# x by tokens and the output through 32x32 squares on VectorE instead of transposes on TensorE, in an attention and FFN kernel on one core

## The reference

```python
h = group_norm(x, 8 groups) * norm_w + norm_b
q, k, v = split(qkv_w @ h + qkv_b)
x = x + proj_w @ (softmax(q^T k / 16) v) + proj_b     # by tokens from here: t = x^T
n = layer_norm(t); u = n / |n|
t = t + softmax((u u^T)^2) @ n
y = layer_norm(t) @ (W - stop(W) + sign(W - mean W)) * mean|W| + bias
out = t + round(clip(y, -1, 1) * 7) / 7                # stored by channels again
```

## Time and profile before

| | |
|---|---|
| median of 3 runs | 1854.93 us (1854.73 to 1854.97) |
| profiled execution: its time, its span | 1856.45 us, 1854.7 us |
| granted TensorE clock | 0.998 of full speed |
| busy share PE, DVE, ACT, POOL | 99%, 68%, 49%, 52% |
| DMA | 35.42 MB, 16415 packets, mean 19 GB/s |

### The profile page before, as it was taken

How to read it: one execution, slowest core, us unless ns; L and a number is a source line. 1 busy time by engine, 2 the same in 40 slices (tenths; PEclk the granted TensorE clock), 3 DMA queues, 4 the chain that set the end, 5 groups by cost and what they waited for, 6 DMA issues and landing times.

```text
span 1854.7 us, 36871 instructions
## 1 busy us (share of the span) xinstructions
PE 1835.7 (99%) x12834; PEld 1699.1 (92%) x12834; DVE 1268.1 (68%) x2516; ACT 906.7 (49%) x1444; POOL 959.6 (52%) x2262
## 2 busy tenths in 40 slices
PE   7999999999999999999999999999999999999997
PEld 6999999989899998999989999999998999989997
DVE  6676766767666676666767667676676766767566
ACT  3545546445463544635446354454544536355452
POOL 0654727457274472734737356372654727447272
PEclk9999999999999999999999999999999999999999
DMA  2000010000100001000010100001000010000000
GB/s 77 1 24 24 1 45 0 23 23 0 45 0 23 23 0 45 0 34 11 0 45 0 45 0 10 35 0 45 0 23 23 0 45 0 23 23 0 24 1 23
DMA packets 16415, 35.42 MB, mean 19 GB/s; under 512 B 2688, under 2 KB 4096, under 8 KB 16384
## 3 DMA queue, kind: packets, MB, share of 16 engines
q1 hardware_dynamic: 16384, 35.01, 5.2%
HBM read 18.23 MB, written 16.78 MB: 19 GB/s over the span
## 4 chain that ended last, share of the span: by engine, by line
PE 98%; DVE 0%; DMA 0%; ACT 0%; SPq 0%; issue 0%; POOL 0%; ACTq 0%; POOLq 0%; DVEq 0%
PE wide L322 35%; PE narrow L424 8%; PE narrow L426 8%; PE narrow L425 8%; PE turn L434 6%; PE wide L424 5%; PE wide L426 5%; PE wide L425 5%; PE narrow L322 5%; PE wide L520 3%; PE turn L481 3%; PE turn L377 2%; PE narrow L452 2%; PE turn L511 1%; PE turn L528 1%; DMA qkv_b_c<-in_L_conv_qkv_b 0%
## 5 line engine op out<-in xcount | busy, mean ns | idle before, releaser
L322 PE MATMUL wide<-xn_hi,prob 128*128 128x512 f32 x1024 | 310.1, 404 | 0.0
L676 ACT ACTIVATE prob<-turn 128x1024 fp32r<-128x1024 f32 x128 | 131.3, 1026 | 322.0 <-PE turn L434 322.0
L1109 POOL TENSOR_TENSOR ln_v<-ln_mv,ln_eps 128x1 f32<-128x1 f32 x256 | 49.3, 193 | 428.8 <-DVE ln_mv L909 251.7
L891 DVE TENSOR_REDUCE neg_max<-wide 128x1 f32<-128x1024 f32 x128 | 156.4, 1222 | 123.0 <-PE wide L322 123.0
L690 ACT ACTIVATE ln<-tok,ln_shift,ln_r 128x256 f32<-128x256 f32 x128 | 77.2, 603 | 319.7 <-POOL ln_shift L1114 319.7
L424 PE MATMUL narrow<-prob 128*128 128x256 f32 x768 | 225.0, 293 | 0.0
L426 PE MATMUL narrow<-prob 128*128 128x256 f32 x768 | 217.0, 283 | 0.0
L425 PE MATMUL narrow<-prob 128*128 128x256 f32 x768 | 216.9, 282 | 0.0
L322 PEld LDWEIGHTS wide<-xn_hi,prob 128*128 128x128 f32 x1024 | 182.8, 188 | 35.4
L896 DVE TENSOR_TENSOR prob<-turn,prob 128x1024 fp32r<-128x1024 f32 x128 | 156.7, 1224 | 61.8 <-ACT prob L676 61.8
L669 ACT ACTIVATE expo<-wide,neg_max 128x1024 f32<-128x1024 f32 x128 | 142.5, 1113 | 58.2 <-DVE neg_max L891 58.1
(11 more groups left out here) (171 smaller groups left out, 5479.1 us busy)
## 6 DMA issues: line engine op xcount, KB each, us to landing
x_raw<-in_x SPq DMA_DIRECT2D x32, 512.0 KB, 3.9
out<-y_sb SPq DMA_DIRECT2D x32, 512.0 KB, 2.8
tok<-in_L_conv_qkv_w SPq DMA_DIRECT2D x1, 768.0 KB, 6.8
ln<-in_L_conv_proj_w SPq DMA_DIRECT2D x1, 256.0 KB, 6.8
ln<-in_L_ffn_weight SPq DMA_DIRECT2D x1, 256.0 KB, 3.0
out_bias<-in_L_conv_proj_b SPq DMA_DIRECT2D x1, 128.0 KB, 3.8
qkv_b_c<-in_L_conv_qkv_b SPq DMA_DIRECT2D x1, 3.0 KB, 7.4
norm_w_c<-in_L_conv_norm_w SPq DMA_DIRECT2D x1, 1.0 KB, 6.1
```

Source lines behind the costliest of these rows:

```text
L322: mm = pe.matmul(o, lhsT, r, start=first and i == 0, stop=last and i == len(parts) - 1)
L676: act.activation(eT_hi[:, n % 2], turn[:, :], ACT.Copy).then_inc(eT_hi_made, 1)
L891: dve.tensor_reduce(neg_max[:, n:n + 1], wide[n % 2][:, :], AX.X, ALU.max, negate=True).then_inc(max_made, 1)
```

## The change

x is no longer turned on TensorE. A second load brings it from DRAM already cut into squares of 32 channels by 32 tokens: partition 32 tq + cc of `x_quad` holds, for channel 32 cb + cc, the tokens 128 n + 32 tq to + 31 of each n. That takes 8 transfers (one for each cb) of 128 KB in rows of 128 bytes. ScalarE adds the bias of the channel (`bias_quad`, 8 instructions a batch, woven into `back`), and VectorE turns all 32x32 squares of half a batch with one transpose (`x_tokens`). The output goes the same way back: the FFN now gives tokens on partitions (its matmuls have the tokens' tile as the stationary side and 256 columns instead of 512), `ffn_out` moves to VectorE, `output` adds `tok` in SBUF and then turns squares into `out_quad`, which lies in the memory of `ln2`; 8 stores of 128 KB in rows of 128 bytes follow. The last batch's output is turned on TensorE (`turn_last`) and stored as before.

The diff, cut to what is spoken of below (`PLACES`, `LAST`: PSUM tiles of the loop and of the last batch):

```diff
+    xq_d = x.rearrange("b (cb cc) (n tq) w -> b tq cc cb n w", cc=Q, tq=P // Q)
+    outq_d = out.rearrange("b (cb cc) (n tq) w -> b tq cc cb n w", cc=Q, tq=P // Q)
...
+        out_quad = ln2[:, :, :].rearrange("p t c -> p (t c)").rearrange("p (cb n tt) -> p cb n tt", cb=C // Q, n=NT)
...
-            def store(f, hf):
-                sp.wait_ge(out_made, 2 * f + hf + 1)
-                sp.dma_start(out_d[f, :, :, hf * HALF:(hf + 1) * HALF], y_sb[:, hf]).then_inc(stored[hf], 16)
+            def load_quads(b):
+                for cb in range(C // Q):
+                    sp.dma_start(x_quad[:, cb], xq_d[b, :, :, cb]).then_inc(quad_loaded, 16)
+
+            def store(f):
+                sp.wait_ge(out_made, 2 * f + 2)
+                for cb in range(C // Q):
+                    sp.dma_start(outq_d[f, :, :, cb], out_quad[:, cb]).then_inc(stored, 16)
+
+            def store_last(hf):
+                sp.wait_ge(last_made[hf], 2)
+                sp.dma_start(out_d[B - 1, :, :, hf * HALF:(hf + 1) * HALF], out_last[:, hf]).then_inc(last_stored, 16)
...
+            load_quads(0)
             def reload(b):
-                sp.wait_ge(xT_up, 2 * b)
                 sp.wait_ge(xn_made, 2 * b)
                 load_x(b)
+            def reload_quads(b):
+                sp.wait_ge(xT_made, 2 * b)
+                load_quads(b)
+
             reload(1)
+            reload_quads(1)
             with sp.Fori(1, B - 1) as b:
                 reload(b + 1)
-                store(b - 1, 0)
-                store(b - 1, 1)
-            for f in (B - 2, B - 1):
-                store(f, 0)
-                store(f, 1)
-            sp.wait_ge(stored[0], 16 * B)
-            sp.wait_ge(stored[1], 16 * B)
+                reload_quads(b + 1)
+                store(b - 1)
+            store(B - 2)
...
-            def x_by_tokens(b, g):
-                if g:
-                    pe.wait_ge(xT_made, 2 * b + 1)
-                for t in range(HT):
-                    for k in range(KC):
-                        mm = pe.transpose(turn[:, t * C + k * P:t * C + (k + 1) * P],
-                                          x_raw[:, k, tile(HT * g + t)], ident[:, :])
-                mm.then_inc(xT_up, 1)
...
             def ffn(f, hf, places=PLACES):
                 pe.wait_ge(ln2T_made, 2 * f + hf + 1)
-                for m in range(KC):
+                for t in range(HT):
+                    o = places["y"][hf][t // 2][:, t % 2 * C:(t % 2 + 1) * C]
                     for k in range(KC):
                         for part in (tokT_lo, tokT_hi):
-                            mm = pe.matmul(places["y"][hf][m], sign_w[:, k, tile(m)],
-                                           part[:, k, hf * HALF:(hf + 1) * HALF],
+                            mm = pe.matmul(o, part[:, k, tile(HT * hf + t)], sign_w[:, k, :],
                                            start=k == 0 and part is tokT_lo, stop=k == KC - 1 and part is tokT_hi)
                 mm.then_inc(y_up, 1)
...
-            def turn_t(f, hf, places=PLACES):
+            def turn_last(hf):
+                pe.wait_ge(sum_made, 2 * (B - 1) + hf + 1)
                 for k in range(KC):
                     for t in range(HT):
-                        mm = pe.transpose(places["tT"][hf][:, k * HALF + t * P:k * HALF + (t + 1) * P],
-                                          tok[:, HT * hf + t, tile(k)], ident[:, :])
-                mm.then_inc(tT_up, 1)
+                        mm = pe.transpose(LAST["sum"][hf][:, k * HALF + t * P:k * HALF + (t + 1) * P],
+                                          y_sb[:, hf, t, tile(k)], ident[:, :])
+                mm.then_inc(last_up, 1)
...
-                    pe.wait_ge(pT_made, (NT - 1) * f + NT - 1)
-                x_by_tokens(b, 0)
-                if f is not None:
                     pe.wait_ge(t2_made, NT * f + NT - 1)
                 queries(b, 0)
-                x_by_tokens(b, 1)
                 if f is not None:
                     pe.wait_ge(t2_made, NT * f + NT)
                 else:
                     pe.wait_ge(prep_dve, 8)
                 queries(b, 1)
                 if f is not None:
-                    pe.wait_ge(xT_made, 2 * b + 2)
+                    pe.wait_ge(pT_made, (NT - 1) * f + NT - 1)
                     turn_ln2(f, 0)
...
-                    turn_t(f, 0)
-                    pe.wait_ge(y_made, 4 * f + 2)
+                    pe.wait_ge(y_made, 2 * f + 1)
                 scores1(b, 0)
                 if f is not None:
-                    pe.wait_ge(out_made, 2 * f + 1)
-                    turn_t(f, 1)
-                    pe.wait_ge(y_made, 4 * f + 4)
+                    pe.wait_ge(y_made, 2 * f + 2)
                 scores1(b, 1)
-                if f is not None:
-                    pe.wait_ge(out_made, 2 * f + 2)
-                else:
-                    pe.wait_ge(xT_made, 2 * b + 2)
                 turn_e1(b, 0)
...
+            def bias_quad(b, cb):
+                if cb == 0:
+                    act.wait_ge(quad_loaded, 16 * QUADS * (b + 1))
+                mm = act.activation(x_quad[:, cb], x_quad[:, cb], ACT.Identity, bias=quad_bias[:, cb, 0:1])
+                if cb == C // Q - 1:
+                    mm.then_inc(quad_biased, 1)
+
+            def layer_norm2(b, n, again=True):
                 act.wait_ge(ln2_scale, NT * b + n + 1)
+                if again and n == 0:
+                    act.wait_ge(stored, 16 * QUADS * b)
...
+                if f is None:
+                    act.wait_ge(quad_bias_made, 1)
+                    for cb in range(C // Q):
+                        bias_quad(0, cb)
...
+                    if more:
+                        bias_quad(b + 1, n)
...
             def x_tokens(b, g):
-                dve.wait_ge(xT_up, 2 * b + g + 1)
-                dve.tensor_tensor(x_tok[:, HT * g:HT * (g + 1), :],
-                                  turn[:, :].rearrange("p (t c) -> p t c", t=HT),
-                                  out_bias[:, :].unsqueeze(1).broadcast_to([P, HT, C]), ALU.add).then_inc(xT_made, 1)
+                dve.wait_ge(quad_biased, b + 1)
+                dve.transpose(x_tok[:, HT * g:HT * (g + 1), :].rearrange("p n (cb cc) -> p n cb cc", cc=Q),
+                              x_quad[:, :, HT * g:HT * (g + 1), :].rearrange("p cb n tt -> p n cb tt")
+                              ).then_inc(xT_made, 1)
...
+            def ffn_out(f, hf, places=PLACES):
+                dve.wait_ge(y_up, 2 * f + hf + 1)
+                wholes = [wide[hf][:, :]] if places is PLACES else places["y"][hf]
+                step = HT // len(wholes)
+                for i, whole in enumerate(wholes):
+                    last = dve.scalar_tensor_tensor(
+                        y_sb[:, hf, i * step:(i + 1) * step], whole.rearrange("p (t c) -> p t c", t=step),
+                        w_mean[:, 1:2], ffn_bias[:, :].unsqueeze(1).broadcast_to([P, step, C]), ALU.mult, ALU.add)
+                last.then_inc(y_made, 1)
...
+            def add_tokens(f, hf):
                 dve.wait_ge(q_made, 2 * f + hf + 1)
-                dve.tensor_tensor(y_sb[:, hf], places["tT"][hf][:, :].rearrange("p (k t) -> p k t", k=KC), y_sb[:, hf],
-                                  ALU.add).then_inc(out_made, 1)
+                dve.tensor_tensor(y_sb[:, hf], tok[:, HT * hf:HT * (hf + 1)], y_sb[:, hf], ALU.add).then_inc(sum_made, 1)
+
+            def output(f, hf):
+
+                add_tokens(f, hf)
+                dve.wait_ge(ln2T_up, 2 * f + 2)
+                dve.wait_ge(sum_made, 2 * f + hf + 1)
+                dve.transpose(out_quad[:, :, HT * hf:HT * (hf + 1)].rearrange("p cb n tt -> p n cb tt"),
+                              y_sb[:, hf].rearrange("p n (cb cc) -> p n cb cc", cc=Q)).then_inc(out_made, 1)
...
-                    output(f, 0)
                 row_max(b, 0)
-                if f is not None:
-                    output(f, 1)
                 row_max(b, 1)
                 e1T_lo(b, 0)
+                x_tokens(b, 0)
                 if more:
                     gn_sums(b + 1, 0)
                 for s in range(1, NT + 1):
@@ -1012,6 +1041,10 @@
                         e1T_lo(b, s)
                     if more and s == 1:
                         gn_sums(b + 1, 1)
+                    if s == 2:
+                        x_tokens(b, 1)
+                    if f is not None and s in (1, 4):
+                        output(f, s // 4)
...
+            ffn_out(f, 0, LAST)
             clip(f, 0)
             ln2T_lo(f, 1, LAST)
             quantise(f, 0)
-            output(f, 0, LAST)
+            ffn_out(f, 1, LAST)
             clip(f, 1)
+            add_tokens(f, 0)
             quantise(f, 1)
-            output(f, 1, LAST)
+            add_tokens(f, 1)
+            for hf in range(2):
+                dve.wait_ge(last_up, hf + 1)
+                dve.tensor_copy(out_last[:, hf, 1], LAST["sum"][hf][:, HALF:N]).then_inc(last_made[hf], 1)
```

(60 more changed lines are left out.)

20 lines of the change are left out of this document (11 added, 9 removed).

## The result

The changed kernel takes **1920.55 us** (1917.36 to 1923.79, 4 runs) against 1854.92: ratio 1.0354, 95% interval 1.0336 to 1.0372, 65.6 us slower, where 15 us faster was forecast. Its profiled execution took 1920.67 us for a span of 1919.0.

What follows compares the result with a forecast made beforehand. TensorE, busy 99% of the span, was taken as the bound; -54.6 (blocks) + 26 (VectorE's wait) + 10 (first batch) + 3.5 (tail) = -15 us gave 1840 us. Own range 1829 to 1850, with other cases 1824 to 2060.

Steps and rivals of the forecast that it cites:

- the sum: Whole kernel: -54.6 + 26 + 10 + 3.5 = -15 us, assuming blocks off TensorE shorten it unless another engine becomes late.
- Blocks, -54.6: TensorE: 62 blocks of 8 transposes leave, 0.88 us each, -54.6 us.
- VectorE's wait, +26: product1(b, 1) waits for residual1(b, 0) behind three new VectorE instructions, 1.75 us in each of 15 fronts, +26 us.
- First batch, +10: Prologue: squares land and ScalarE starts 8 biases at 39.5 us, first exponential at 44.5, +10 us.
- the prediction's own sign of being wrong: First batch: the prediction is wrong if the first exponential starts much before 44 us.
- Tail, +3.5: From the last FFN matmul's end to the last sum's end: 8.5 us instead of 5.0, +3.5 us.
- Transfers hidden: Rows of 128 bytes in the loop: 13 ns each on 4 engines, 53 us a batch, hidden with 18 us of room, 0.
- the prediction's count: Latest landing of a batch's stores before TensorE wants ln2: 926.8 us in the prediction, 1026.7 on e6's clock.
- slow rows: Rival: squares' rows slower than 17.5 ns, so the stores hold up ScalarE's back; decides from 17.8 ns; chance 0.35.
- dear transposes: Rival: a VectorE transpose takes 2.3 us, +35 and up to 10 more in step 4, 1875 to 1885 us; chance 0.10.
- The forecast of 1840: Whole kernel: 1854.9 - 15 = 1840 us, transfers hidden and VectorE's one wait; 1829 to 1850, chance 0.40.

Runs made afterwards that it cites:

- e6: Changed kernel with 28 more idle wait instructions on TensorE ahead of its first matmul: 1832.98 us.
- e9: e6 with the output's transposes moved to steps 3 and 5 (sums stay) and x_tokens(b, 0) put between row_max(b, 0) and row_max(b, 1): 1809.19 us.
- e8: e6 with output(f, 0) and output(f, 1) in steps 3 and 5 instead of 1 and 4: 1808.69 us.
- e11: e6 with 12 more loads of squares between a batch's eight loads and eight stores: 2029.6 us.
- e2: Changed kernel with 16 more idle wait instructions on TensorE ahead of its first matmul: 1925.33 us.
- e5: Changed kernel with 20 more idle wait instructions on TensorE ahead of its first matmul: 1924.49 us (2 runs).
- e10: e6 with 6 more loads of squares between a batch's eight loads and eight stores: 1833.47 us.
- e1: Changed kernel with 96 more idle wait instructions on TensorE ahead of its first matmul: 1837.38 us.
- e4: Changed kernel with each batch's eight loads and eight stores cut into rows of 1 KB, values in the wrong order: 1919.54 us.
- e3: Kernel before the change with 144 more idle wait instructions on TensorE ahead of its first matmul: 1905.38 us.
- e7: Changed kernel with 174 more idle wait instructions on TensorE ahead of its first matmul: 1864.5 us (1844.95 to 1870.99).

## Why the prediction was wrong, step by step

Starts of `product2` in the traces give a ledger (us; the end is that of the span):

| | first `product2` | period in the loop | last period | last `product2` to the end |
|---|---|---|---|---|
| before | 101.63 | 114.01 | 113.62 | 43.2 |
| after | 101.06 | 119.0 | 110.28 | 47.6 |
| e6 | 102.72 | 112.33 | 110.28 | 46.7 |
| e9 | 99.71 | 110.69 | 110.29 | 47.6 |

- **The step that failed** is the sum, by the sentence it starts from: "a block taken off TensorE shortens the kernel by its own length, as long as nobody else becomes late". Somebody did who is on no list of engines: TensorE's own instruction stream. Two blocks are 32 instructions out of the prologue (33 with a wait that went too), and the body's start moved from some 9 behind a block's border to 24 ahead of it. The sum has no term for that. From the first to the last `product2` the kernel after takes 1770.3 us and e6 1682.8: the missing term is **+87.4 us**, 6.7 a jump (the medians of the runs differ by 87.6). 51.1 of it are the waits. The other 36.3 go with the clock: it was at half in the loop for 12 stretches of 6.8 us and one of 3.4, 85 in all, of which some 19 are the second waits; half of the remaining 66 is 33, by my estimate.
- e6 starts 1.7 us later than the kernel after (102.72 against 101.06). Its 28 instructions are not the cause: e8, e9 and e11 have them too, and start at 99.7 to 100.1.
- The views that I read could have shown the risk only in part: the kernel before has 19 fetches on its page and none in its loop, which says that the body stays in place, but not by how little. The count of instructions would have said that some half of a block was left; where the borders lie took e2, e5 and e6 to find.
- *The instructions that stay.* In e6 no packet of `q8` comes between 206.1 us, 7.7 ahead of the loop's first branch back at 213.8, and 1680.9, 6.8 behind its last at 1674.1: seven blocks and one ahead, eight, stay through 13 jumps. In the kernel after, whose body touches eight, nine come a turn. The border lies between 20 and 28 more instructions.
- *Blocks, -54.6.* Right. The last period, which has no other difference, falls by 3.33 for four blocks: 0.83 a block, not 0.88, and -51.6 for 62.
- *VectorE's wait, +26.* Right in place and cause, a little large: 14 waits, not 15, since the last front has no group norm sums ahead; the period without it is 110.69 (e9), with it 112.33: 1.64 each, +23. By the medians e8 gained 24.3 us over e6, e9 23.8; the loop gives 23 of either, and the rest is no more than starts and ends differ by. The transpose takes 1.24 us (the earlier trace rows gave 1.22 for the sum of that size). That this term and the gain of the blocks are each 3 us too large is luck: together they were forecast at -28.6 and measured at -28.6.
- *First batch, +10.* Wrong: nothing that stands out of the scatter of the start. By the times of their packets the squares' rows ran from 9.9 to 30.7 us, where I had the landing at 39.5. In the kernel after the biases started at 32.06, right behind the last values, took 3.30 us, and the exponential followed at 35.62: the prediction's own sign of being wrong, an exponential much before 44 us. I had 0.63 us a bias for 0.41, and 13 ns a row after row, where the rows run closer (below). The first `product2` starts at 101.06 after, at 99.7 to 102.7 in e6, e8, e9 and e11, and at 101.63 - 1.7 for two blocks = 100.0 before. Part of the scatter is the clock, whose record sets in at the higher level at 18.3 us after and at 14.9 before. The same eight matmuls, after and before:

```profile
15.10 3.53 PE L375 MATMUL wide<-expo,tok 128*128 128x256 f32 x8
```

```profile
15.54 1.97 PE L347 MATMUL wide<-expo,tok 128*128 128x256 f32 x8
```

- *Tail, +3.5.* 46.7 to 47.6 against 43.2: +3.5 to +4.4.
- *Transfers hidden.* Right, with the room where it was put. A batch's rows take 43.5 us in e6 (forecast 53), 61.6 in e10 and 82.3 in e11, by the times of their packets. Counted from their start in e6, 953.7, they end at 1015.3 in e10 and 1036.0 in e11: before the 1026.7 us of the prediction's count, and 9.3 behind it, which is the wait that TensorE has in e11. That four DMA engines share such a transfer, each with a row every 13 ns, was the author's estimate: no run shows an engine's share, only the whole, 16384 rows in 43.5 us or 2.7 ns a row, where the forecast's 53 us are 3.2. The rivals of slow rows and dear transposes did not happen: in e6 a load's packet lasts 13.0 ns on the average and a store's 18.2, and a transpose 1.24 us.

Without the missing term the sum of measured terms is -51.6 + 23 + 0 + 3.5 = -25. e6's span is 22.4 us below that of the kernel before, and 2.6 of the difference are its later start (102.72 against 100.1 in e8 and e11). The forecast of 1840 would have been 10 us high, because of the first batch.

## What to carry to other kernels

When an edit adds or removes instructions ahead of or inside a long loop, compare the number of packets on the queue of instructions and look at the first instructions behind the jump; a wait there that is put down to an engine done before, or to nothing, was a fetch here. Then shift the loop by some tens of idle instructions before judging the edit: here that was worth 87 us, more than the whole change. And on an engine that feeds the busiest one, what stands ahead of the value wanted matters, not its total load: three instructions moved made 23 us.

## What was not expected of the hardware

- TensorE's loop body of 1654 or 1688 instructions is kept from turn to turn when it touches seven blocks of 256 by the count (19 packets in all before and in e6, 20 in e1), and brought again whole, nine fetches of 16 KB each turn, when it touches eight (136 after and in e2, e4, e5). A miss costs a wait of 2.5 us (32.5 us for 13 in e4), and a second one if the jump lands near a block's end (1.5 us with 24 instructions left, in e4, 2.3 with 8, in e2; with 4 the two are one wait of 5.4, in e5). Three of the nine waits in e3 and the two in e7 are longer, 3.9 us on the average; there the packets of two blocks start within 0.4 us of each other.
- With the body's end 12 instructions into the eighth block 2 of 13 jumps missed in the profiled execution (e7), with some 49 nine of 13 (e3), with over 90 all of them (after, e2, e5).
- Behind those waits the granted clock is 0.50 for 3.4 or 6.8 us (after, e3), behind the 9 us waits of e11 for 10.2. In e3, with waits of 2.9 us on the average, the loop has it five times for nine misses.
- Rows of 128 bytes in both directions pass faster than their own durations one after another. Windows of loads and of stores in e6, DMA share and GB/s last:

```profile
954.00:970.00 16.00, 16.00 (x114) 14.78 (x113) 12.21 (x24) 8.83 (x15) 11.02 (x32) 1.00 0.34 54
974.00:996.00 22.00, 22.00 (x165) 21.09 (x164) 14.41 (x36) 14.74 (x28) 17.76 (x46) 1.00 0.40 44
```

  54 GB/s are 0.42 rows a nanosecond, one every 2.4 ns over all engines, 9.5 ns an engine if four share them; a load's packet lasts 13 ns. By the times of the packets never more than 8 of them are under way at once in e6, while of the 4 KB rows of x up to 20 are. That fits four engines with two packets each, by my estimate, but a packet's engine is not in the trace, so it is not resolved: the issue table gives no landing time for these transfers, while it gives 2.2 us for those of 1 KB rows in e4. Nor is it settled whether the rows or SyncE's issuing sets the pace, for its queue needs as long (17.69 us for eight loads).
